# A chain of fp32 low-rank and dense products on one core: a reordered first product, and finished tiles of the last product added on GpSimd

## The reference

```
x = x + (x @ B0[id0[b]].T) @ A0[id0[b]].T      # rank 16
x = x + x @ W + (x @ A1[id1[b]].T) @ B1[id1[b]]  # W is 2048 x 2048, rank 16
```

## Time and profile before

| | us |
|---|---|
| median of 3 runs | 1315.17 |
| lowest and highest | 1312.83, 1318.78 |
| the profiled execution | 1315.14 |
| its span in the trace | 1313.4 |
| PE busy | 1296.6 (99%) |
| DVE busy | 957.0 (73%) |
| ACT busy | 458.7 (35%) |
| POOL busy | 161.5 (12%) |

### The profile page before, as it was taken

One profiled execution on the slowest core, in us unless ns is written; L12 is line 12 of the kernel. 1 busy time (PEld: TensorE's weight loads), 2 busy tenths in 40 slices (PEclk: granted clock), 3 DMA queues, 4 the chain that ended last, 5 costly groups with the idle time before them and its releaser, 6 DMA issues.

```text
span 1313.4 us, 15493 instructions
## 1 busy us (share of the span) xinstructions
PE 1296.6 (99%) x5716; PEld 1069.7 (81%) x5716; DVE 957.0 (73%) x1031; ACT 458.7 (35%) x540; POOL 161.5 (12%) x277
## 2 busy tenths in 40 slices
PE   8999999999999999999999999999999999999998
PEld 6888888888888888888888888887878888888876
DVE  4436866556684776876777866769898887778988
ACT  3332232222334432332232443334433344444441
POOL 3000130021023210001201100111000111100011
PEclk9999999999999999999999999999999999999999
DMA  8875876668999955668968573572965987867467
GB/s 282 282 260 199 281 263 232 231 215 303 361 358 245 298 205 204 221 201 298 366 235 311 175 257 112 193 255 101 261 219 201 371 265 205 232 168 247 121 201 200
DMA packets 87549, 316.33 MB, mean 241 GB/s; under 512 B 15650, under 2 KB 15650, under 8 KB 81074
## 3 DMA queue, kind: packets, MB, share of 16 engines
q1 hardware_dynamic: 61010, 246.44, 54.2%
q0 software_dynamic: 26464, 68.90, 18.8%
HBM read 213.48 MB, written 102.83 MB: 241 GB/s over the span
## 4 chain that ended last, share of the span: by engine, by line
PE 85%; DVE 8%; DMA 3%; issue 2%; ACT 1%; POOLq 0%; POOL 0%; DVEq 0%; SPq 0%; ACTq 0%
PE ps L1342 42%; PE ps L2512 33%; PE ps L1293 3%; PE ps L2468 2%; PE ps L1251 2%; DVE xq L2243 1%; DVE b_lo L2262 1%; PE ps L1272 1%; DMA out_y<-stage 1%; DMA x_raw<-in_W 1%; DVE w_lo L2256 1%; PE ps L2454 1%; DMA out_y<-stage_all 1%; DVE uq L2287 1%; DVE xq L2230 1%
## 5 line engine op out<-in xcount | busy, mean ns | idle before, releaser
L1342 PE MATMUL ps<-b_hi,w_hi 128*128 128x512 f32 x888 | 346.8, 391 | 3.4 <-DVE b_lo L982 3.0
L1342 PE MATMUL ps<-b_lo,w_hi 128*128 128x512 f32 x888 | 346.1, 390 | 0.0
L1342 PE MATMUL ps<-b_hi,w_lo 128*128 128x512 f32 x888 | 346.0, 390 | 0.0
L2512 PE MATMUL ps<-b_hi,w_hi 128*128 128x512 f32 x784 | 305.8, 390 | 3.6 <-DVE w_lo L2256 1.8
L2512 PE MATMUL ps<-b_hi,w_lo 128*128 128x512 f32 x784 | 305.1, 389 | 0.0
L2512 PE MATMUL ps<-b_lo,w_hi 128*128 128x512 f32 x784 | 305.1, 389 | 0.0
L1342 PEld LDWEIGHTS ps<-b_hi,w_hi 128*128 128x128 f32 x888 | 167.1, 188 | 39.4 <-issue 3.4
L1342 PEld LDWEIGHTS ps<-b_hi,w_lo 128*128 128x128 f32 x888 | 167.1, 188 | 35.0
L1342 PEld LDWEIGHTS ps<-b_lo,w_hi 128*128 128x128 f32 x888 | 167.2, 188 | 34.7
L2512 PEld LDWEIGHTS ps<-b_hi,w_hi 128*128 128x128 f32 x784 | 147.2, 188 | 36.5 <-DVE w_lo L2256 3.0
L2089 ACT CAST w_hi<-wq 128x1024 fp32r<-128x1024 f32 x98 | 103.3, 1054 | 207.9 <-PE ps L2512 195.0
(11 more groups left out here) (186 smaller groups left out, 1284.1 us busy)
## 6 DMA issues: line engine op xcount, KB each, us to landing
x_raw<-in_xT SPq DMA_DIRECT2D x56, 512.0 KB, 6.8
wq<-w_ops SPq DMA_DIRECT2D x28, 1024.0 KB, 4.9
w_raw<-in_W SPq DMA_DIRECT2D x55, 512.0 KB, 6.0
xq<-in_xT SPq DMA_DIRECT2D x44, 512.0 KB, 6.3
out_y<-stage POOLq DMA_DIRECT2D x38, 512.0 KB, 5.5
w_sum<-x_raw SPq DMA_DIRECT2D x24, 512.0 KB, 8.9
out_y<-stage_all POOLq DMA_DIRECT2D x48, 256.0 KB, 6.1
wq<-w_sum SPq DMA_DIRECT2D x12, 1024.0 KB, 7.5
```

What stands on the lines that cost most here:

```text
L1342: last = pe.matmul(bank[:, :], w[n % 2][:, c, t * P:(t + 1) * P], x[:, 2 * j + c, :], start=(j == 0 and c == 0 and w is w_hi and x is b_hi ...
L2512: last = pe.matmul(out, w[:, h, c, col:col + P], b[x], start=(po in (Q1, Q2, Q5, Q3) and c == 0 and i == 0), stop=(c == 3 and i == 2), ski ...
```

## The change

There are three groups of edits.

1. Start and P1. SP issues the weight tile before the x tile, and waits before u = 3 for the inner low-rank weights (`in_loaded`) instead of A0. ACT and DVE split the weight before the x tile in the first units as they do later. PE's first unit waits for the high part of x only, and takes the passes in the order hi*hi, then w_lo, then b_lo. The first `in_mm` slot moves behind `p_mm` of unit 1.
2. S3 in P1. `w_second` of unit n is done by DVE in unit n + 1, behind the splits, its store follows one unit later, and `load_a21` is issued ahead of `load_raw`.
3. M5. The four adds of C11 and C22 are done by POOL on a semaphore of their own, `pool_fin_done`. Those of C12 stay on DVE. On POOL the add stands ahead of the store of `stage`.

```diff
@@ sync
-                sp.wait_ge(a0_loaded, 16 * NB)
+                sp.wait_ge(in_loaded, 32)
+            load_raw(u)
             load_x(0, X11, u)
-            load_raw(u)
...
+            if 2 <= n + 2 < UNITS:
+                load_a21(n + 2)
             if RAWS <= n + RAWS < FIRST:
                 load_raw(n + RAWS)
             if n < 0 or p == 0:
-                if 2 <= n + 2 < UNITS:
-                    load_a21(n + 2)
...
-            if 0 <= n < UNITS:
-                sp.wait_ge(postsum_done, n + 1)
-                store_sum(S3, n)
+            if 0 < n <= UNITS:
+                sp.wait_ge(postsum_done, n)
+                store_sum(S3, n - 1)
@@ scalar, and the same in vector
-            if n < 1 and due:
-                x_split(*due)
             if n + 1 < LAST:
                 w_split(n + 1)
-            if n >= 1 and due:
+            if due:
                 x_split(*due)
@@ vector
-                if 0 <= n < UNITS:
-                    w_second(n)
+                if 0 < n <= UNITS:
+                    w_second(n - 1)
@@ tensor, first_unit
-            pe.wait_ge(x_ready, 1)
-            for w, x in ((w_hi, b_hi), (w_hi, b_lo), (w_lo, b_hi)):
+            pe.wait_ge(x_hi_done, 1)
+            for w, x in ((w_hi, b_hi), (w_lo, b_hi), (w_hi, b_lo)):
                 if w is w_lo:
                     pe.wait_ge(w_ready, 1)
+                if x is b_lo:
+                    pe.wait_ge(x_ready, 1)
@@ tensor
-                if n == 1 and t == 3:
-                    in_mm(0, 0, (0,))
...
+            if n == 1:
+                in_mm(0, 0, (0,))
@@ two_level
+    def by_pool(c):
+
+        return c in (C11, C22)
...
+        def fin(c, h):
+            pair = slice(2 * h, 2 * h + 2)
+            pool.wait_ge(*quarter_done(M5, c, 2 * h + 1))
+            pool.wait_ge(*quarter_done(M3, c, 2 * h + 1))
+            pool.wait_ge(*sides(M5, c, h, False))
+            pool.tensor_tensor(uq[:, c, pair, :], uq[:, c, pair, :], stage[:, GROUP[M5][c], pair, :], ALU.add
+                               ).then_inc(pool_fin_done, 1)
+            pool.wait_ge(pool_fin_done, pool_fin_no[c, h])
+
         def store_fin(c, h):
 
-            pool.wait_ge(fin_done, fin_no[c, h])
+            if not by_pool(c):
+                pool.wait_ge(fin_done, fin_no[c, h])
...
                 if finish(n):
+                    if by_pool(finish(n)[0]):
+                        fin(*finish(n))
                     store_stage(M5, *finish(n))
                     store_fin(*finish(n))
...
-                if finish(n):
+                if finish(n) and not by_pool(finish(n)[0]):
                     fin(*finish(n))
```

More of the change, by code:

```diff
@@ L1590, in two_level @@
     fin_no = {}
+    pool_fin_no = {}
     for n in range(LAST + 1):
         if finish(n):
-            fin_no[finish(n)] = len(fin_no) + 1
+            table = pool_fin_no if by_pool(finish(n)[0]) else fin_no
+            table[finish(n)] = len(table) + 1
     for t, _ in LAST_PARTS:
@@ L1698, in two_level @@
     fin_done = sem("fin_done")
+    pool_fin_done = sem("pool_fin_done")
     lr_less_done = sem("lr_less_done")
```

## The result

The changed kernel takes a median of 1315.82 us (1313.63 to 1317.40, 20 runs), the kernel before 1312.31 us (1310.62 to 1318.78, 20 runs). The ratio is 1.0021, with a 95% interval of 1.0013 to 1.0029. So the change makes the kernel slower, by 2.8 us in the ratio and by 3.5 us between the medians. The forecast was 2.5 us faster.

A forecast was written before the change was run, and what follows sets the result against it. PE, busy 99% of the span, was taken to bound the kernel, so time is won only where it idles or runs at the lower clock. 1315.1 - 6.2 (start) + 3.7 (adds on POOL) = 1312.6 us, range 1306.0 to 1316.5.

The forecast's parts named there:

- The start: P1, edits 1 and 2: unit 3 starts at 31.5 instead of 37.73, 6.2 us won (bounds 4.5 and 6.6).
- The hold: M5: DVE splits with two SBUF inputs stand for POOL's whole 2.3 us add; sum +3.7 us (bounds -1.1 and +5.5).
- Hindrance, against none: M5, POOL beside DVE: +3.7 us if they hinder each other; rival (a), no hindrance, -1.1, total 1307.8, 30%.
- The estimate of 2.25 us for the add: POOL's 128x1024 add in M5: half of 4497 ns for 2048 columns; the forecast took 2.3 us.
- C22's part, +2.5: M5: DVE stands 1.8 us at each of two w_lo, less 1.1 for a removed add; together +2.5 us.
- the term of C11, +1.2 "between 0 and 3": M5, w_lo of unit 5: 2.3 us if POOL wins, or a later store; taken at +1.2 us, between 0 and 3.
- The low clock behind a wait: P1 behind the wait before unit 2: 34 matmuls take 9.30 us at clock 0.83, 7.7 at full clock.
- Rival (c): M5: delayed C11 stores make ACT's cast for C22 wait 10 us longer instead of 1.2; total 1321.4, chance 6%.
- The sign: Whole kernel: 1312.6 us against 1315.1; chances 0.27 faster, 0.68 within 0.5%, 0.05 slower.

The follow-up runs named there:

- experiment 10: Edit 1 alone on the kernel before, with w_second and its stores and loads at their old places, all adds on DVE: 1315.15 us, ratio 1.0019.
- experiment 9: Edit 2 alone (w_second behind the splits, A21's load ahead of the weight's) on the kernel before: 1308.31 us, ratio 0.9971.
- experiment 4: Changed kernel with POOL's add left out and POOL writing zeros twice over uq in its place: 1310.18 us, ratio 0.9973 to the kernel before.
- experiment 8: Changed kernel with POOL copying stage to uq (one SBUF input) instead of adding: one run, 1314.18 us.
- experiment 12: Changed kernel with POOL adding one tile at a time, eight adds of 128x512: 1315.48 us, ratio 1.0018 to the kernel before.
- experiment 5: Changed kernel with POOL's stage store ahead of the add, ACT waiting for the add before writing C22: 1314.26 us, ratio 1.0010 to the kernel before.
- experiment 7: Changed kernel with only C22's two adds on POOL and C11's on DVE: 1309.46 us, ratio 0.9982 to the kernel before.
- the start alone: Changed kernel with the four adds put back on DVE, so edits 1 and 2 only: 1306.87 us, ratio 0.9953 to the kernel before.
- experiment 2: Edit 3 alone (four adds on POOL) on the kernel before, start and S3 as before: 1321.14 us, ratio 1.0051.

## Why the prediction was wrong

**The start: right in its steps, a little high in size.** Measured, with the forecast in brackets: PE from 8.26 (8.3), in_stk's cast at 18.02 (18.0 for the arrival), the A21 tile at 26.6 (26), b_lo of unit 3 at 30.1 (29.4), unit 3 at 32.00 (31.5), 5.7 us earlier (6.2). One thing was not seen. The A0 tiles landed 3 us later, at 17.34 and not 14.20; PE idled 0.2 us for it. The next w and x tiles after the first four loads now go out at 11.07 and not 12.70, beside the last A0 tile at 11.79. That this is the cause was not tested. That edit 1 loses without edit 2 (experiment 10) was in the working: edit 2 "is what gives unit 2 its parts without the A21 tile". Edit 2 alone is worth 3.8 of the 6.2 us (experiment 9).

**The hold: right in kind.** POOL's add ran 2.2 to 2.4 us, 2.3 forecast. Hindrance, against none, was the forecast's choice, and experiments 4, 8 and 12 show how it goes here: a DVE op with two SBUF inputs and a POOL op that reads SBUF take turns whole, one that only writes isn't concerned. That is what the Trainium skill (SBUF — State Buffer, Who interferes with whom) states, and the runs agree: w_lo 3.39 us beside the add, 1.22 beside the memset. Its further words, that whoever issues first has the ports, fit all rows but one: in experiment 5 a w_lo recorded as begun 0.42 us ahead of the add ran behind it. The estimate of 2.25 us for the add, half of the figure in the Trainium skill (GPSIMD Engine Reference, Elementwise side-by-side), is near the measured 2.38. C22's part, +2.5, was measured at +2.5 (experiment 7), with each w_lo held for 1.8 us as forecast. It is right against the start alone; in the changed kernel itself the waits of units 9 to 11 grew by 1.8 us.

**What failed: the term of C11, +1.2 "between 0 and 3".** By the two profiles it is 6.9 - 2.5 = 4.4 us, and 6 to 7 against the start alone (experiment 7). What the runs show in its place:
- POOL won the race for w_lo of unit 5. That was in the text at 2.3 us and was taken at half, since "DVE's idle time and the two missing adds give some back". PE's wait grew by 2.2 us. A delay that ends on an operand PE is waiting for can't be given back by slack that DVE has later. It should have stood in full. Every profile with C11's whole adds on POOL has this wait: 2.98 us here, 2.97 in experiment 2, 2.91 in experiment 5, and only 0.82 with the memset.
- The low clock behind a wait. I took 1.6 us of it as a gain where the wait of 3.0 us at the start went, and put no price on it where my own sum made a new wait of the same length. In the profiled execution it cost 1.6 us at unit 5 and 1.5 us from 1290.6 to 1294.0, 3.1 us in all, nearly the whole of 6.9 - 3.7. It can't be the whole story of the median: in experiment 2 no low clock follows the same wait, and the three executions of the changed kernel without any took as long. What they lose by stays open.
- The store. Rival (c) made ACT wait 10 us longer for it. In the changed kernel ACT waits 2.80 us where it was 3.67, and to issue the store ahead of the add gains 1.5 us (experiment 5). The landing can cost more: in experiments 2, 4 and 8 ACT waits 6.45, 6.88 and 7.41 us for it. Why the store takes so long isn't shown.

**The sign.** In the profiled executions the changed kernel is 0.6 us above before (spans 1314.0 and 1313.4). The rest of the 2.8 us lies in the base: the first three runs of the kernel before had a median of 1315.17, as the profiled execution, and 20 runs have 1312.31. The absolute 1312.6 was meant as 2.5 us faster; by 1312.31 it reads as none. The time, 1315.82, lies inside the range of 1306.0 to 1316.5, but the way it moved was wrong.

## What to carry to other kernels

Work moved from VectorE to GpSimd is no relief when it reads SBUF and VectorE is busy with two-input SBUF ops: here each add took 1.1 us from DVE and held it for 1.8 to 2.2. Where TensorE is 99% busy, price a new wait in full, and give the low clock that may follow it a chance and a price (here nothing or 1.6 us), just as one does for the wait that goes. When two delays end on the same engine, expect them to overlap: to take one away can bring out the other. And measure the parts of a change apart: this one hid some 6 us of gain behind 9 us of loss.

## What the runs showed of the hardware that was not expected

- The low clock came after a single wait of 1.9 us (experiment 12, excess 3.75 us at unit 5) as after one of 3.0. In experiment 7 PE waited 2.3 us before unit 11, and its profile shows no slow stretch behind. In experiment 2 it waited 2.97 us for the same w_lo as in the changed kernel, and the clock stayed at 1.00. In the changed kernel the slow matmuls of 1290.6 to 1294.0 begin 1.5 us after PE was at work again, behind waits of 0.95, 1.48 and 2.28 us. What tells these apart stays open.
- An accumulating store of 512 KB took 6.0 us from issue to landing when issued alone (1240.22) and 9.9, 12.8 or 16.4 us when it went out behind other POOL transfers. While the one of 12.8 us was under way in the kernel before, the DMA engines moved 104 GB/s from 1258 to 1260 and 232 to 414 GB/s from 1260 to 1266. Why it took so long is open.
- A POOL op that is held has its wait inside its duration: the same add is shown with 4.24 us when a DVE op was under way and with 2.38 when not.
- A POOL copy of 128x1024 from SBUF to SBUF took 1.04 us, two memsets of that size 1.97, an add 2.38.
